# The shares of a token's four experts, worked out in the tile stage instead of between routing steps, and a mask column written for two batches at once

## The reference

```python
router_logits = x @ gate_w.T
scores = jax.nn.sigmoid(router_logits)
_, topk_ids = jax.lax.top_k(scores + e_bias[None, :], K)          # K = 4 of E = 32
topk_w = jnp.take_along_axis(scores, topk_ids, axis=1)
topk_w = topk_w / jnp.sum(topk_w, axis=1, keepdims=True)          # the shares
a = silu(einsum(x, w1)) * einsum(x, w3) * combine[:, :, None]     # combine holds the shares
out = einsum(a, w2)
```

```python
V = (values @ Wv).reshape(...) * ind_v[:, None, :, None]
attn = softmax(scores) * ind_k[:, None, None, :]
attn = attn / where(sum(attn) == 0, 1, sum(attn))
```

## Time and profile before

| | |
|---|---|
| runs | 1332.86, 1331.65, 1340.57 us (median 1332.86) |
| the profiled execution | 1333.14 us, of which the span is 1331.3 |
| busy | PE 951.9, PEld (weight loads) 719.2, DVE 717.0, ACT 572.6, POOL 616.5 us |
| routing stage, 311 to 543 us | groups 25 to 28 us apart |
| tile stage, 544 to 680 us | 48 pairs, about 2.6 us apart |

### The profile page before, as it was taken

The page is one execution under the profiler, slowest core; times in us unless marked ns, Lnnn a source line. Parts: engine busy times, 40 slices in busy tenths (PEclk is TensorE's granted clock), DMA queues, the critical chain, the costliest instruction groups (busy, mean ns, idle before and its releaser), DMA issues. The chain is left out here.

```text
span 1331.3 us, 27306 instructions
## 1 busy us (share of the span) xinstructions
PE 951.9 (71%) x10334; PEld 719.2 (54%) x10334; DVE 717.0 (54%) x1742; ACT 572.6 (43%) x960; POOL 616.5 (46%) x582
## 2 busy tenths in 40 slices
PE   1477877875657664399942287868777788996898
PEld 1356666653222221399940176757566677886465
DVE  3465555435567647255543464645555566653565
ACT  1156666664565554266631132322323233332454
POOL 1267666662677666144447714425251502111354
PEclk9998788865787877699975687979797989999899
DMA  4221111105656756777765104040404131100001
GB/s 137 74 69 51 50 50 50 50 2 178 232 208 202 277 204 246 202 201 203 203 194 199 44 7 141 24 148 16 146 17 144 27 131 65 66 2 1 9 25 33
DMA packets 112065, 144.04 MB, mean 108 GB/s; under 512 B 14325, under 2 KB 93090, under 8 KB 105794
## 3 DMA queue, kind: packets, MB, share of 16 engines
q1 hardware_dynamic: 73026, 110.68, 24.5%
q0 software_dynamic: 8192, 16.79, 4.2%
q10 hardware_dynamic: 30720, 14.82, 3.9%
HBM read 76.60 MB, written 65.40 MB: 107 GB/s over the span
## 5 line engine op out<-in xcount | busy, mean ns | idle before, releaser
L438 POOL TENSOR_TENSOR p_lo_a<-probs_a,p_hi_a 128x1024 f16<-128x1024 f32 x64 | 136.3, 2130 | 87.4 <-ACT p_hi_a L297 87.2
L1470 POOL DMA_INDIRECT rows_x<-rows_r,index_r x128 | 138.0, 1078 | 71.4 <-issue 36.7
L917 POOL DMA_INDIRECT fetched_a<-rows_y,chosen_row x128 | 123.1, 961 | 49.7 <-issue 37.3
L617 PEld LDWEIGHTS psum<-v_x_a,probs_a 128*128 128x128 f32 x1024 | 131.1, 205 | 3.4 <-issue 0.3
L617 PE MATMUL psum<-v_x_a,probs_a 128*128 128x65 f32 x1024 | 132.0, 286 | 0.0
L923 POOL TENSOR_TENSOR vareps_a<-meanvar_a,eps 128x4 f32<-128x4 f32 x8 | 1.6, 201 | 244.3 <-DVE meanvar_a L830 244.3
L795 DVE TENSOR_REDUCE negmax_a<-psum 128x8 f32<-128x1024 f32 x64 | 78.2, 1223 | 67.4 <-remote 45.5
L1648 POOL TENSOR_TENSOR h_lo_t<-hidden_t,h_hi_t 96x512 f16<-96x512 f32 x48 | 55.4, 1154 | 93.9 <-ACT h_hi_t L1616 93.9
L354 DVE TENSOR_REDUCE negmax_a<-psum 128x8 f32<-128x1024 f32 x64 | 78.3, 1223 | 22.0 <-PE psum L168 21.7
L296 ACT ACTIVATE probs_a<-psum 128x1024 f32<-128x1024 f32 x64 | 65.6, 1024 | 45.7 <-PE psum L152 45.6
L662 PE MATMUL psum<-ident,att_a 128*128 128x128 f32 x256 | 44.4, 297 | 44.5 <-issue 27.4
(11 more groups left out here) (336 smaller groups left out, 3084.0 us busy)
## 6 DMA issues: line engine op xcount, KB each, us to landing
values<-v_out_r SPq DMA_DIRECT2D x16, 1040.0 KB
v_x_a<-values SPq DMA_DIRECT2D x16, 1040.0 KB
keys<-k_out_r SPq DMA_DIRECT2D x16, 1024.0 KB
listed_t<-rows_x SPq DMA_DIRECT2D x96, 128.0 KB, 2.3
rows_y<-result_t ACTq DMA_DIRECT2D x48, 256.0 KB, 2.3
k_a_a<-keys SPq DMA_DIRECT2D x16, 512.0 KB
k_b_a<-keys SPq DMA_DIRECT2D x16, 512.0 KB
q_pad_a<-narrow_q SPq DMA_DIRECT2D x64, 64.0 KB
```

What stands on the lines that cost most here:

```text
L438: nc.gpsimd.tensor_tensor(p_lo[:, s % RING0, :], probs[:, s % NPR, :], p_hi[:, s % RING0, :], ALU.subtract).then_inc(s_plo, 1)
L617: last_ = nc.tensor.matmul(PV[:, part, i * (HD + 1):(i + 1) * (HD + 1)], probs[:, s % 3, lane(part, i)], v_x[:, par, b % GB, h, :], start= ...
L917: nc.gpsimd.indirect_dma_start(fetched[:, b % NF1, k, :], None, rows_y, bass.IndirectOffsetOnAxis(ap=chosen["row"][:, b, k:k + 1], axis=0) ...
L1470: nc.gpsimd.indirect_dma_start(rows_x, bass.IndirectOffsetOnAxis(ap=index[:, g * GB + t, k:k + 1], axis=0), rows[:, g % 2, t, :, :].rearra ...
```

## The change

The three `same` instructions leave `choose`. `slot`, `slots` (now kept for all 32 batches) and `comb` (likewise) move to memory that outlives the routing stage, and a function `share(g, step)` in the tile stage does one of the three instructions after DVE's product of pair q: for q = 13 + 4 g + step, so after pairs 13, 14, 15, 17, 18, 19, and so on to 43. The pairs between them (16, 20, 24) are the ones that already carry a weight's lower half. The semaphore waits behind `comb` and ahead of `slots` go with them. On ACT, the mask column is written twice per group for two batches each, with a broadcast input, instead of four times for one batch; the constant `unit` that it was made from goes.

```diff
@@ experts0
+    slot, comb = sb("slot", [P, B, E0]), sb("comb", [P, B, E0])
+    slots = sb("slots", [P, B, 8])
...
@@ keep, on ScalarE
-                            if half_ == 0:
-                                nc.scalar.activation(v_out[:, t // 2, t % 2, :, D1], const["unit"][:, :], ACT.Copy,
-                                                     scale=const["mask"][:, b:b + 1])
+                            if n % 4 == 0:
+                                nc.scalar.activation(v_out[:, t // 2, :, :, D1],
+                                                     const["mask"][:, b:b + 2].unsqueeze(2).broadcast_to([P, 2, H]), ACT.Copy)
...
@@ choose, on VectorE
-                    after(nc.vector.tensor_tensor(comb[:, :, :], earned[:, :, :],
-                                                  total[:, :].unsqueeze(2).broadcast_to([P, GB, E0]), ALU.mult))
+                    nc.vector.tensor_tensor(comb[:, g * GB:(g + 1) * GB, :], earned[:, :, :],
+                                            total[:, :].unsqueeze(2).broadcast_to([P, GB, E0]), ALU.mult)
...
-                    if g:
-                        dve.wait_ge(s_index, g)
...
-                    wide = [P, GB, K0, E0]
-                    after(nc.vector.tensor_tensor(same[:, :, :, :], at.unsqueeze(2).broadcast_to(wide),
-                                                  slots[:, :, 0:K0].unsqueeze(3).broadcast_to(wide), ALU.is_equal))
-                    after(nc.vector.tensor_tensor(same[:, :, :, :], same[:, :, :, :],
-                                                  comb[:, :, :].unsqueeze(2).broadcast_to(wide), ALU.mult))
-                    after(nc.vector.tensor_reduce(chosen["share"][:, g * GB:(g + 1) * GB, :], same[:, :, :, :], AX.X, ALU.add))
...
@@ the tile stage, on VectorE
+                def share(g, step):
+                    wide, batches = [P, GB, K0, E0], slice(g * GB, (g + 1) * GB)
+                    if g or step:
+                        dve.wait_ge(s_same, 3 * g + step)
+                    if step == 0:
+                        last_ = nc.vector.tensor_tensor(same[:, :, :, :], slot[:, batches, :].unsqueeze(2).broadcast_to(wide),
+                                                        slots[:, batches, 0:K0].unsqueeze(3).broadcast_to(wide), ALU.is_equal)
+                    elif step == 1:
+                        last_ = nc.vector.tensor_tensor(same[:, :, :, :], same[:, :, :, :],
+                                                        comb[:, batches, :].unsqueeze(2).broadcast_to(wide), ALU.mult)
+                    else:
+                        last_ = nc.vector.tensor_reduce(chosen["share"][:, batches, :], same[:, :, :, :], AX.X, ALU.add)
+                    last_.then_inc(s_same, 1)
...
+                    g, step = divmod(q - 13, 4)
+                    if 0 <= g < G and step < 3:
+                        share(g, step)
```

More of the change, by code:

```diff
@@ L1046, in experts0 @@
         mark = rt("mark", [P, 2, GB, E0], F16)
-        earned, total, comb = rt("earned", [P, GB, E0]), rt("total", [P, GB]), rt("comb", [P, GB, E0])
+        earned, total = rt("earned", [P, GB, E0]), rt("total", [P, GB])
         group_sum, so_far = rt("group_sum", [P, E0]), rt("so_far", [P, G + 1, E0], F16)
-        placed, slot = rt("placed", [P, GB, E0]), rt("slot", [P, B, E0])
-        slots, index = rt("slots", [P, GB, 8]), rt("index", [P, B, K0], U32)
-        same = rt("same", [P, GB, K0, E0])
+        placed, index = rt("placed", [P, GB, E0]), rt("index", [P, B, K0], U32)
         pad_row = rt("pad_row", [1, E0], I32)
@@ L1368, in choose @@
                     after(nc.vector.tensor_tensor(at, placed[:, :, :], chose, ALU.mult))
-                    if g:
-                        dve.wait_ge(s_index, g)
                     for t in range(GB):
-                        last_ = nc.vector.max(slots[:, t, :], slot[:, g * GB + t, :])
+                        last_ = nc.vector.max(slots[:, g * GB + t, :], slot[:, g * GB + t, :])
                     after(last_)
-                    nc.vector.tensor_single_scalar(index[:, g * GB:(g + 1) * GB, :], slots[:, :, 0:K0], -1.0,
+                    nc.vector.tensor_single_scalar(index[:, g * GB:(g + 1) * GB, :], slots[:, g * GB:(g + 1) * GB, 0:K0], -1.0,
                                                    ALU.add).then_inc(s_index, 1)
-                    wide = [P, GB, K0, E0]
-                    after(nc.vector.tensor_tensor(same[:, :, :, :], at.unsqueeze(2).broadcast_to(wide),
-                                                  slots[:, :, 0:K0].unsqueeze(3).broadcast_to(wide), ALU.is_equal))
-                    after(nc.vector.tensor_tensor(same[:, :, :, :], same[:, :, :, :],
-                                                  comb[:, :, :].unsqueeze(2).broadcast_to(wide), ALU.mult))
-                    after(nc.vector.tensor_reduce(chosen["share"][:, g * GB:(g + 1) * GB, :], same[:, :, :, :], AX.X, ALU.add))
                 def split(n, views):
@@ L1487, in experts0 @@
         raw_last, raw_gate, raw_pick = tl("raw_last", [P, 3, NF]), tl("raw_gate", [P, E1]), tl("raw_pick", [P, CHUNKS, P])
-        s_last, s_last_hi = tsem("last"), tsem("last_hi")
+        s_last, s_last_hi, s_same = tsem("last"), tsem("last_hi"), tsem("same")
+        same = tl("same", [P, GB, K0, E0])
         uppers = [(raw_last[:, n, :], last[name][0][:, :]) for n, name in enumerate(("w1", "w3", "w2"))]
@@ L1796, in program @@
             "ident": sb("ident", [P, P]), "power": sb("power", [P, 1]), "ones": sb("ones", [P, P]), "eps": sb("eps", [P, 1]),
-            "mask": sb("mask", [P, B]), "unit": sb("unit", [P, H]),
+            "mask": sb("mask", [P, B]),
             "low_comb1": sb("low_comb1", [32, 1]),
@@ L1843, in _ @@
                 nc.vector.memset(const["eps"][:, :], EPS)
-                nc.vector.memset(const["unit"][:, :], 1.0)
                 nc.vector.memset(const["ones"][:, :], 0.0).then_inc(const["s_power"], 1)
```

## The result

The changed kernel took a median of 1376.88 us in four runs (1368.69 to 1385.70), the kernel before 1334.86 in four. The ratio is 1.031, with an interval of 1.024 to 1.039. Its profiled execution took 1368.69 us, of which the span is 1366.9. That lies far above my range, and on the side to which I had given 3%.

A forecast was written before the change was run, and what follows sets the result against it. PE bounds the tile stage; in routing no engine is near full and a group-to-group chain decides. Routing gives 7.0 + 0.2 + 0.2 = 7.4 us, the tile stage costs nothing: 1333.14 - 7.4 = 1325.7, predicted median 1325.5, range 1318 to 1334.

The forecast's parts named there:

- the side to which I had given 3%: Whole kernel: slower by more than one per cent (over 1346 us), needing the tile stage to pay full price; chance 3%.
- Tile stage costs nothing: Tile stage: 24 instructions of about 0.72 us hide in DVE's 1.31 us idle per pair; cost nothing, upper bound 17.3 us.
- POOL's `h_lo` never met a `share` step with two inputs: Tile stage: they miss each other by 0.26 and 0.54 us; rival that they collide, up to 1343 us, 10%.
- Wide mask column: ACT, routing: 16 more elements cost 0.01 us; columns ahead of v2 give 0.2 us in all; rival that it is slow, 2%.
- `lower_rows` earlier: Routing, groups 0 to 6: without `same`, `lower_rows` starts earlier, by 0.22 to 1.93 us in the groups shown; 7.0 us in sum.
- The rule: Routing: new `lower_rows` starts at s - 0.20 + 0.63 + 1.20 = s + 1.63, s being ACT's old start of k0.
- the 1.6 among my signs: Routing, sign of being right: `lower_rows` starts about 1.6 us after ACT's k0.
- The step that failed: Routing: after `lower_rows` comes a chain of waits to the next `index`, so its gain, 7.0 us, brings groups forward.
- My first rival: Routing: each group loses again what it won, through unexplained waits; only about 1 us remains, 1332 us; chance 17%.

The follow-up runs named there:

- late set: Runs on one chip beside the program before, in which TensorE's results come late against its records; the program before takes 1331 to 1336 us.
- on-time: Set or trace in which TensorE's results come with its records; the program before takes 1234 us.
- the shares alone: Changed program with the three instructions moved to the tile stage, but the mask column written as before: 1228.3 us, ratio 0.995 to the program before.
- theory D: Scatters hold TensorE's results back between logits and last k chunk; run: changed program, 12 of each group's 16 scatters moved behind the last group, 1322.9 us.
- the shares back: Changed program with the three instructions back in `choose`, wide mask column and buffer places kept: 1236.4 and 1235.9 us on-time, 1336.2 us in a late set.
- the stores behind: Changed program with all 32 stores of keys and values behind the last group: 1456 us in a late set, not comparable; `index(7)` at 552.9.
- the mask alone: Program before with only the mask column written for two batches at once from a broadcast input: 1236.2 us, ratio 1.003, on-time.

## Why the prediction was wrong, step by step

- **Tile stage costs nothing:** right, with its mechanism and its pitch. POOL's `h_lo` never met a `share` step with two inputs; three of the eight sums (L1631, one input) started 0.06 us before it ended, and it stayed at 1.15 to 1.16 us.
- **Wide mask column:** 0.26 us for 32 elements, against 0.32 for 16: right in kind. Alone it gave nothing measurable.
- **`lower_rows` earlier:** it gave 4.4 us over the seven groups instead of 7.0, for two reasons. The rule took k0 on ACT 0.20 us earlier in every group, 1.4 in all; measured from `index`, k0 starts 0.4 later in sum (20.5 against 20.1), which is 1.8 of the 2.6 missing. The other 0.8 is the way from k0 to `lower_rows`: the rule gives 1.83 us behind the new k0 (0.63 + 1.20; the 1.6 among my signs left the 0.20 out). Measured it is 1.88 in six groups and 2.27 in group 4, where k0 starts at 451.11 and `lower_rows` at 453.38, because ACT's rounding waited 0.36 us for a scatter of two groups earlier.
- **The step that failed** stands between the working and the sum: "so a `lower_rows` that comes earlier brings the next group forward." I let the chain behind it take as long as before. In a late set it doesn't: the phase went from 45.2 to 84.0 us in sum. My first rival named the place ("waits that nothing I can name explains"), but priced it at most as a gain lost. Those waits were already in the trace of before: 26.4 us of idle ahead of ACT's k copies, 8.4 of it "remote". The row of before (64 copies, idle before them and what ended it):

```profile
L1271 ACT ACTIVATE k_out_r<-psum 128x512 f16<-128x512 f32 x64 | 37.5, 599 | 26.4 <-PE psum L1163 14.6 <-remote 8.4 <-issue 3.0
```

The same in the on-time trace of the shares alone:

```profile
L1271 ACT ACTIVATE k_out_r<-psum 128x512 f16<-128x512 f32 x64 | 37.6, 597 | 8.5 <-PE psum L1163 7.0
```

And in the changed kernel:

```profile
L1271 ACT ACTIVATE k_out_r<-psum 128x512 f16<-128x512 f32 x64 | 37.9, 596 | 48.0 <-remote 38.1 <-PE psum L1163 6.5 <-issue 2.7
```

The same copies, 38 us of work each time, and 26.4, 8.5 and 48.0 us of idle. A wait that nothing explains can grow, and I should have given it a price on both sides.

**What is shown:** in late sets the loss comes from moving the three instructions, while in an on-time set moving them costs nothing; it is lateness of TensorE's results between the logits and k7; and with the shares moved, it goes with 8 matmuls fewer and comes back with 16 idle instructions. Neither the place of the buffers, nor the mask column, nor the stores, nor the pause ahead of the logits makes it alone. **What stays open** is how the three instructions in `choose` held it down. In the six groups of before with the shorter phases (5.4 to 7.0), PE takes 6.6 us or more from the start of v3 to that of k3, in the changed program mostly 5.5 to 5.8; but a pause behind k3, which brings the distance from v3 to the logits to 9.7 us, as much as before (9.6), cured nothing. Whether the pause has to lie ahead of k3 wasn't tried. Fewer scatters in a late set (theory D) weren't tried either, nor idle instructions in the program before.

In the on-time sets the shares alone give 0.5%, close to the 0.55% of my forecast (7.4 of 1333). That is in part luck, since the balance there is another: the groups come 22.6 us apart on average (20.7 to 25.4), and POOL hardly waits for `index`: 14.4 us in 2 waits, nearly all of it the first group's, against 34.7 in 8. With 12 of a group's 16 scatters away, the seven periods fall from 158.1 to 149.2 us. So POOL most likely takes back a part of what the shares give; what is left is 158.1 against 161.7 and 164.2 in the two traces with the shares back. The changed kernel itself never ran in an on-time set, so its own time there isn't measured.

## What to carry to other kernels

A wait that the profile can't explain ("remote", "issue") isn't a fixed cost that moves along with the chain; price it up as well as down before you bring work closer together. Run the kernel before beside every experiment and look at its absolute time: here, in conditions 8% apart, the change lost 3.1% in one and its main part, the shares alone, gained 0.5% in the other. To tell instructions from work, put idle instructions in the place of the work.

## What the runs showed of the hardware

- **TensorE's results can be late by up to 11 us** against the records of its matmuls, in steps of about 0.71 us: the chunks k4 to k7 of the run with the stores behind come 2.14, 2.82 and 2.81 us apart, while three matmuls of 512 columns take 1.28 us at a granted clock of 0.5. In the four traces of the changed program the granted clock is 1.00 when each of these phases begins and 0.50 in its last microsecond; but even a phase that starts at 0.50 in an on-time trace lasts only 4.3 to 5.7 us, so the clock alone doesn't make 15.
- **VectorE stalls in the same steps.** Thirty-two MAX8 in a row, which wait for nothing, DVE's timeline in the program before (late):

```profile
526.85 1.50 DVE L1444 MAX8 raw_r<-raw_r 128x8 f32<-128x32 f32 x15
529.05 0.19 DVE L1444 MAX8 raw_r<-raw_r 128x8 f32<-128x32 f32 x1 [0.70 <-issue]
530.45 0.20 DVE L1444 MAX8 raw_r<-raw_r 128x8 f32<-128x32 f32 x1 [1.21 <-issue]
531.85 0.20 DVE L1444 MAX8 raw_r<-raw_r 128x8 f32<-128x32 f32 x1 [1.21 <-issue]
```

  And with the shares alone (on time):

```profile
503.66 3.07 DVE L1436 MAX8 raw_r<-raw_r 128x8 f32<-128x32 f32 x32
```

  After 15 short instructions in a row six come 0.7 to 1.4 us after the one before, then they flow again. All 11 late traces have six or seven such stalls, none of the 9 on-time traces has one. It is the quickest sign of which kind a trace is.
- **Late traces are also incomplete.** They hold 10,600 to 11,400 semaphore events, on-time traces 15,020 to 15,050 for nearly the same program. Most of the missing ones are landings of DMAs, and they are missing in the stages where the time is lost: in the routing stage 619 of them in the trace of before against 2,393 with the mask alone, and behind the tile stage 1,154 against 2,970 (also between the two, where no time is lost but the stalls above: 608 against 1,056), but in the first attention 2,534 in both and in the tile stage 2,106 against 2,112. That and the dependence on mere instruction count suggest that it is the recording of instructions that stalls the engines: short instructions make records faster than they leave. The Trainium skill ("NOTIFIC — the notification-queue block", section "7.1 Overflow: three behaviours, one of which stalls the engine") says that the block which writes these records holds its producers back when its internal pipeline fills, which would fit the stalls, though not by itself the missing events. It was not tested. The times of the runs around the traced ones agree with theirs; if those runs were not recorded in the same way, this explanation falls. The other thing that goes by the number of instructions is their loading. Its packets of 16 KiB take a median of 0.99 to 1.09 us in the late traces and 0.98 to 1.06 in the on-time ones, at most 2.0 in both, so the loading itself isn't slower.
- **The lateness isn't the routing stage's alone.** From the first gather of the second attention to the last output it is 641.0 us in the trace of before, 640.3 in the changed one and 566.6 in the on-time trace of the shares alone. The change doesn't touch it.
